# Attention, layer norm and a routed feed-forward on one core: three loads moved, a gate's weights packed, a layer norm's statistics and scaling moved

## The reference, cut to what matters

```python
def _L0_attn_ref(x, Wq, bq, Bq, Aq, ...):          # x is (2, 1024, 512), 16 heads of 32
    q, k, v = lora_linear(x, ...) for each          # x @ W + b + 0.5 * (x @ B) @ A
    attn = softmax(q @ k / sqrt(32), axis=-1)
    return lora_linear(attn @ v, Wo, bo, Bo, Ao)

def _moe(x, Wg, W1, W3, W2, sw1, sw3, sw2):        # 2048 tokens, 8 experts, 256 slots each
    probs = softmax(xt @ Wg); eidx = argmax(probs); gate = probs[eidx]
    pos = place of the token among those of its expert; keep = pos < 256
    h = silu(xd @ W1) * (xd @ W3); oe = h @ W2      # per expert, on the tokens it holds
    out = oe of the token's slot * gate * keep
    return out + silu(xt @ sw1) * (xt @ sw3) @ sw2  # the shared expert, on all tokens

x = layernorm(x + attn(x))
x = layernorm(x + moe(x))
```

## Time and profile before

| | |
|---|---|
| time, median of three runs | 1094.25 us (1091.41 to 1097.25) |
| the profiled execution | 1093.02 us, its span 1091.4 us |
| busy | PE 1041.3 us (95%), DVE 724.1 (66%), ACT 557.3 (51%), POOL 540.3 (50%) |
| granted TensorE clock, mean | 0.989 of full speed |
| chain that ended last | PE 78%, DVE 7%, DMA 4%, issue 4%, ACT 4%, SP's queue 2% |

### The profile page before, as it was taken

One profiled execution on the slowest core, in us unless ns is written; L12 is line 12 of the kernel. 1 busy time (PEld: TensorE's weight loads), 2 busy tenths in 40 slices (PEclk: granted clock), 3 DMA queues, 4 the chain that ended last, 5 costly groups with the idle time before them and its releaser, 6 DMA issues.

```text
span 1091.4 us, 16143 instructions
## 1 busy us (share of the span) xinstructions
PE 1041.3 (95%) x5586; PEld 726.8 (67%) x5586; DVE 724.1 (66%) x1194; ACT 557.3 (51%) x978; POOL 540.3 (50%) x294
## 2 busy tenths in 40 slices
PE   6999999999999999999999988968999999999996
PEld 5777555455555545556445567756899999998884
DVE  5549878878687787888887576512476666664154
ACT  4311556656466565666665654411355656664116
POOL 2100788889878898788889830370000000003600
PEclk9999999999999999999999999989999999999998
DMA  7964342724337142332641492350277777765704
GB/s 265 306 180 136 83 112 56 174 65 95 78 78 175 49 111 55 78 97 51 169 154 63 124 287 72 117 139 18 70 211 214 215 239 229 222 201 125 112 1 154
DMA packets 163765, 146.79 MB, mean 134 GB/s; under 512 B 42529, under 2 KB 126753, under 8 KB 163440
## 3 DMA queue, kind: packets, MB, share of 16 engines
q1 hardware_dynamic: 157040, 129.97, 42.8%
q0 software_dynamic: 6656, 15.93, 5.3%
HBM read 85.75 MB, written 35.67 MB: 111 GB/s over the span
## 4 chain that ended last, share of the span: by engine, by line
PE 78%; DVE 7%; DMA 4%; issue 4%; ACT 4%; SPq 2%; ACTq 0%; DVEq 0%
PE bank L812 16%; PE bank L964 13%; PE bank L977 11%; PE bank L912 11%; PE bank L900 8%; PE bank L1109 8%; PE bank L1022 4%; PE bank L872 3%; PE bank L989 3%; DMA raw<-in_L_ffn_W_dram 2%; DVE w2lo L1735 1%; DVE mx L1606 1%; DMA bcol<-in_L_attn_bk_dram 1%; PE bank L819 1%; DVE sa L1742 1%
## 5 line engine op out<-in xcount | busy, mean ns | idle before, releaser
L1336 ACT ACTIVATE prob<-bank 128x512 f32<-128x512 f32 x512 | 289.9, 597 | 194.3 <-PE bank L964 186.3
L1606 DVE TENSOR_REDUCE mx<-bank 128x1 f32<-128x512 f32 x512 | 324.9, 680 | 81.5 <-PE bank L912 78.6
L740 POOL TENSOR_TENSOR psum<-psum,prob 128x1024 f32<-128x1024 f32 x156 | 366.8, 2388 | 1.0 <-ACT prob L1336 1.0
L964 PE MATMUL bank<-Qs,Ks 97*128 97x512 f32 x512 | 209.0, 424 | 0.9 <-DMA Qs<-mrow 0.9
L912 PE MATMUL bank<-Ks,Qs 96*128 96x512 f32 x512 | 184.6, 405 | 3.8 <-DVE mx L1606 1.3
L964 PEld LDWEIGHTS bank<-Qs,Ks 97*128 97x128 f32 x512 | 94.3, 188 | 106.3 <-ACT prob L1336 74.3
L791 POOL DMA_DIRECT2D oe_d<-oe_sb x16 | 8.8, 548 | 248.8 <-ACT oe_sb L1474 247.8
L977 PE MATMUL bank<-prob,V 128*32 128x512 f32 x1024 | 131.4, 602 | 0.0
L912 PEld LDWEIGHTS bank<-Ks,Qs 96*128 96x128 f32 x512 | 97.2, 190 | 50.2 <-DVE mx L1606 21.8
L740 POOL TENSOR_TENSOR psum<-prob,prob 128x1024 f32<-128x1024 f32 x32 | 76.0, 2394 | 67.8 <-ACT prob L1336 37.8
L900 PE MATMUL bank<-xThi,Wsl 128*128 128x512 f32 x256 | 99.6, 400 | 3.8 <-DMA bcol<-in_L_attn_bk_dram 3.1
(11 more groups left out here) (251 smaller groups left out, 2067.9 us busy)
## 6 DMA issues: line engine op xcount, KB each, us to landing
raw<-in_L_ffn_W_dram SPq DMA_DIRECT2D x120, 256.0 KB
Ks<-plane_khi SPq DMA_DIRECT2D x64, 128.0 KB, 2.7
Qs<-plane_qhi SPq DMA_DIRECT2D x64, 128.0 KB, 2.3
raw<-in_L_ffn_sw_dram SPq DMA_DIRECT2D x30, 256.0 KB
xin<-in_L_attn_x_dram SPq DMA_DIRECT2D x16, 256.0 KB, 5.0
v_d<-v_sb POOLq DMA_DIRECT2D x16, 256.0 KB, 3.9
Wsl<-wt_d SPq DMA_DIRECT2D x16, 256.0 KB, 4.7
Ks<-plane_klo SPq DMA_DIRECT2D x32, 128.0 KB, 2.5
```

Of the source, the lines that this page charges most:

```text
L740: po.tensor_tensor(psum[:, pr], (prob[0] if kc == 1 else psum)[:, pr], prob[kc % RING][:, pr], ALU.add).then_inc(sem("sum_done"), 1)
L964: nc.tensor.matmul(score_at(v, i), Ks[v.b][0:97, hh, kc * P:(kc + 1) * P], Qs[v.b][0:97, hh, v.hf * HALF:(v.hf + 1) * HALF], start=True, s ...
L1336: ACTV(prob[kc % RING][:, hh, :], score_at(v, i), ACT.Exp, scale=SCALE).then_inc(sem("exp_done"), 1)
L1606: ins = RED(mx[(hf + ahead) % 2][:, 4 * hh + qt, part:part + 1], src, AX.X, ALU.max)
```

## The change

There are three edits.

1. `load_slot` for the next group is no longer issued by SP in slot 1, behind pair 1, the load of V and the store of the attention output, but in slot 0, between pair 0 and the row of maxima.
2. The gate's weights are one tile `wgp` of 128 columns: the high part in columns 0 to 7, the low part in columns 8 to 15. `logits` is two matmuls for each of four blocks (turned tile high, turned tile low), 8 in place of 12, into 16 rows; the logits are transposed with 16 columns per tile, and VectorE adds the two parts (one operation more).
3. Statistics of tiles 8 to 11 are taken by VectorE behind the remainders of the turned tiles 0 to 7 and no longer between the residual adds; `x1` of tiles 8 to 15 is done by VectorE and no longer by ScalarE; and the turned tiles 0 to 7 go through five banks and no longer three.

```diff
@@ wgp
-    wgp = [gate(f"wgp{s}", [P, DC, P], FR) for s in ("hi", "lo")]
-    lgT = gate("lgT", [E, T], F32)
+    wgp = gate("wgp", [P, DC, P], FR)
+    lgT = gate("lgT", [2 * E, T], F32)
@@ x1_bank
-        return bank[(2, 3, 5)[t % 3]]
+        return bank[(2, 3, 5, 6, 7)[t % 5] if t < NT // 2 else (2, 3, 5)[t % 3]]
@@ SP: stack_unit, half
             stack(b, 0, 0)
             if v is not None:
+                group = v.g + v.h // 4
+                if v.slot == 0 and group < NG - 1:
+                    load_slot(value((group + 1) * P))
                 next_mrow(v)
...
-            elif v.proj and v.slot == 1:
-
-                c, need = value((v.g + 1) * P), value(v.projected())
-                sp.wait_ge(sem("pj_done"), need)
-                load_slot(c)
@@ GpSimd
-        for s in range(2):
-            po.memset(f32(wgp[s][:]), 0.0).then_inc(sem("wgp_zero"), 1)
+        po.memset(f32(wgp[:]), 0.0).then_inc(sem("wgp_zero"), 1)
@@ TensorE: turn_x1, logits
                 pe.wait_ge(sem("x1_rdy"), t + 1)
-                if t >= 3:
-                    pe.wait_ge(sem("x1_lo"), t - 2)
+                if t == 4:
+                    pe.wait_ge(sem("at_done"), 4 * NG + 1)
+                if t >= 5:
+                    pe.wait_ge(sem("x1_lo"), t - (4 if t < NT // 2 else 2))
                 turn(x1_bank(t), rows(t)).then_inc(sem("x1_t"), 1)
...
-            pe.wait_ge(sem("x1_lo"), 4 * i + 4)
+            pe.wait_ge(sem("x1_lo"), max(4 * i + 4, 5))
             if i >= 2:
                 pe.wait_ge(sem("lg_ev"), i - 1)
-            elif i == 0:
-                pe.wait_ge(sem("at_done"), 4 * NG + 1)
-            split3(bank[6 + i % 2], lambda a, dc: wgp[a][:, dc, :],
-                   lambda p, dc: xT[p][:, dc, i * 512:(i + 1) * 512]).then_inc(sem("lg_full"), 1)
+            for dc in range(DC):
+                for p in range(2):
+                    mm = nc.tensor.matmul(bank[6 + i % 2], wgp[:, dc, :], xT[p][:, dc, i * 512:(i + 1) * 512],
+                                          start=dc == 0 and p == 0, stop=dc == DC - 1 and p == 1)
+            mm.then_inc(sem("lg_full"), 1)
...
-            mm = nc.tensor.transpose(bank[6][:, t * E:(t + 1) * E], lgT[:, t * P:(t + 1) * P], ident[0:E, 0:E])
+            mm = nc.tensor.transpose(bank[6][:, 2 * t * E:2 * (t + 1) * E], lgT[:, t * P:(t + 1) * P], ident[0:2 * E, 0:2 * E])
@@ ScalarE
-        x1_hi(3, 4)
+        x1_hi(3, 8)
         root(2, 8, 12)
-        x1_hi(4, 8)
-        x1(2, 8, 12)
         take_logits(0)
         conv(13, 0, 0, None)
         x1_hi(8, 11)
         root(3, 12, NT)
         x1_hi(11, 12)
-        x1(3, 12, NT)
         take_logits(1)
@@ VectorE
+        def x1(k, start, stop):
+
+            ve.wait_ge(sem("ln_shift"), k)
+            for t in range(start, stop):
+                TS(rows(t), rows(t), ln_scale[:, t:t + 1], ln_shift[:, t:t + 1], ALU.mult,
+                   ALU.add).then_inc(sem("x1_rdy"), 1)
...
-        nc.vector.tensor_copy(r3["lg"][:], by_t(bank[6])).then_inc(sem("lg_read"), 1)
+        parts = bank[6][:, 0:2 * NT * E].rearrange("p (t s e) -> p t s e", s=2, e=E)
+        nc.vector.tensor_copy(r3["lg"][:], parts[:, :, 1]).then_inc(sem("lg_read"), 1)
         ve.wait_ge(sem("lg_read"), 1)
+        TT(r3["lg"][:], parts[:, :, 0], r3["lg"][:], ALU.add).then_inc(sem("lg_read"), 1)
+        ve.wait_ge(sem("lg_read"), 2)
```

More of the change, by code:

```diff
@@ L1382, in wgp_split @@
         def wgp_split():
-            ac.wait_ge(sem("wgp_zero"), 2)
+            ac.wait_ge(sem("wgp_zero"), 1)
             ac.wait_ge(sem("wg_ld"), 16)
-            ACTV(wgp[0][:, :, 0:E], wg_raw[:], ACT.Identity).then_inc(sem("wgp_hi"), 1)
+            ACTV(wgp[:, :, 0:E], wg_raw[:], ACT.Identity).then_inc(sem("wgp_hi"), 1)
         def x1_hi(start, stop):
@@ L1392, in take_logits @@
             ac.wait_ge(sem("lg_full"), i + 1)
-            ACTV(lgT[:, i * 512:(i + 1) * 512], bank[6 + i % 2][0:E, :], ACT.Copy).then_inc(sem("lg_ev"), 1)
+            ACTV(lgT[:, i * 512:(i + 1) * 512], bank[6 + i % 2][0:2 * E, :], ACT.Copy).then_inc(sem("lg_ev"), 1)
         def conv(kind, c, sets, need):
@@ L1690, in tile, with statistics @@
             TT(rows(t), o_bank(t), xr[t % 4][:], ALU.add).then_inc(sem("y_done"), 1)
+            if t // 4 != 2:
+                statistics(t)
+        def statistics(t):
             ve.wait_ge(sem("y_done"), t + 1)
@@ L1750, in _ @@
             tile(t)
-        variances(8, 12)
         x1_rest(0, 3)
         ve.wait_ge(sem("wgp_hi"), 1)
-        TT(wgp[1][:, :, 0:E], wg_raw[:], f32(wgp[0][:, :, 0:E]), ALU.subtract).then_inc(sem("wgp_lo"), 1)
-        x1_rest(3, 4)
+        TT(wgp[:, :, E:2 * E], wg_raw[:], f32(wgp[:, :, 0:E]), ALU.subtract).then_inc(sem("wgp_lo"), 1)
+        x1_rest(3, 8)
+        for t in range(8, 12):
+            statistics(t)
+        variances(8, 12)
         scales(2, 8, 12)
-        x1_rest(4, 8)
+        x1(2, 8, 12)
         for t in (12, 13):
@@ L1766, in _ @@
         scales(3, 12, NT)
+        x1(3, 12, NT)
         x1_rest(11, NT)
```

## The result

| | before | after |
|---|---|---|
| time, median of six runs | 1094.9 us (1091.41 to 1097.25) | 1086.47 us (1082.96 to 1087.57) |
| ratio | | 0.991 [0.9887, 0.9933] |
| the profiled execution, its span | 1093.02, 1091.4 us | 1086.6, 1085.0 us |
| TensorE busy | 1041.3 us (95%) | 1038.3 us (96%) |
| at tile 11's residual add | 641.84 | 637.70 |

8.4 us less between the medians; the forecast was 1084, its range 1078.5 to 1090.5. The last three lines read as a ledger of the two profiled executions: the lead is 4.14 us at the end of attention, 6.88 at the shared expert's first chunk, 8.76 at the transposition of the logits, and 6.4 at the end. The profiled execution of the kernel before was 1.9 us quicker than its median and that of the change was at its median, so the 8.4 of the medians and the 6.4 of the spans do not contradict each other.

A forecast was written before the change was run, and what follows sets the result against it. TensorE, busy 95% of the span, was taken as the bound. 4.8 + 1.8 + 3.0 = 9.6 us off 1093.02 (profiled) or 1094.25 (median) gave 1083.4 or 1084.7, forecast 1084; 8-in-10 range 1078.5 to 1090.5.

The forecast's parts named there:

- rival (a): VectorE/GpSimd port collisions cost full price (0.7) and TensorE's clock falls ahead of `up(0, ...)` (about 1.3): 1086; chance 0.14.
- Edit 1, 4.8: Attention, slot 1: moving the slices removes TensorE's bias waits, 4.0 us in group 1 and 0.8 in group 2.
- SP's delay of 0.1: SP's queue, slot 0: six moved issues against 3.9 us of slack delay what follows by 0.1 us, hidden.
- Rival (b): SP is held up in the new place: 3 x 2.9 = 8.7 us lost, 1093, no change; chance 0.06.
- Edit 2, 1.8: Gate logits: fewer matmuls save 1.9 us in TensorE's lone stretch, less 0.1 for transpositions; VectorE's extra operation hidden.
- Edit 3 with logits 0 and 1, 3.0: Between attention and routing: VectorE's new order starts the shared expert's first chunk 3.0 us earlier.
- the dear one: Behind attention: scales and scalings on VectorE both wait for GpSimd's adds, leaving 2.3 us won at the first chunk.
- a sign of being wrong: VectorE behind attention: scalings or scales of over 1 us each beside GpSimd's adds would show the forecast wrong.
- between the last two: First chunk's gain: 3.0 us, chosen between 3.4 (only small scale operations wait) and 2.3 (scalings wait too).
- The port: VectorE and GpSimd block each other at a shared port pair; by it scalings collide and the sum uses 2.3.
- What follows moves as a whole: Shared expert and experts, behind routing: they start earlier by the whole gain; the 28.5 us of ScalarE waits taken unchanged.
- Rival (c): Gain of the gate and VectorE-order edits is hidden by VectorE's delay or ScalarE's waits: 1089; chance 0.09.

The follow-up runs named there:

- gate_only: Kernel before with only the gate's low-part weights made eight more columns of one tile (fewer logits matmuls): 1093.15 us, 0.9982.
- add15_behind: Changed kernel with GpSimd's residual add for tile 15 waiting until VectorE has scaled tiles 8 to 11: one run, 1089.96 us.
- slices_only: Kernel before with only the next group's weight slices issued in slot 0 instead of slot 1: 1092.4 us, 0.9982.
- order_only: Kernel before with only the late statistics, scalings of tiles 8 to 15 on VectorE and five banks: 1091.2 us, 0.9968.
- scale8_act_conv_late: Changed kernel with scaling of tiles 8 to 11 back on ScalarE and a VectorE conversion moved behind tile 14: 1082.25 us, 0.9887.
- no_gate_scatter: Changed kernel without the 16 indirect DMAs that write the gates, so the gates are zero: 1068.86 us, 0.9757.
- before_gates_in_norm: Kernel before without the gates' scatter, full result through row scaling by 1/gate and the layer norm: 1077.72 us, 0.9994 on the third chip.

## Why the prediction was right

The time was 1086.5 where 1084 was forecast, 8.4 us won where 9.6 were summed. The ledger of the two traces has 8.76 for the same sum. The time is nearest to rival (a), 1086, and half of that rival came: the port collisions took their full price. Its other half, a further fall of the clock that would make `up(0, ...)` slower, didn't (its first 24 matmuls take 5.59 us, 0.233 each), so that the time agrees with (a) is in part luck. By the steps:

- **Edit 1, 4.8.** The first wait and the slow clock behind it gave 4.0 us (15.33 against 19.35), and the second 1.0, the predicted 4.0 and 0.8. At the end of attention only 4.14 stand. In between, TensorE's timeline shows two short idle times for which no releaser is seen: 1.27 us ahead of 324.82, where it was 0.81 before, and 0.89 ahead of 519.13, where nothing was. They were not foreseen, and the edit alone isn't their cause: gate_only, which doesn't have it, shows both, and longer. With them the term is 0.7 short in the two traces, the largest miss of the sum. In the medians it may be more: the prediction took the wait's price from one execution in which the clock fell behind it, and in two of the four traced kernels without the edit it doesn't, where the term is 3.0 to 3.4 and not 4.8. The 2.3 measured for the edit alone, up to 3.8 by its interval, fits that; how often the clock falls there isn't known from four traces. SP's delay of 0.1 was 0.16, hidden as said; six issues cost 4.1 us (3.95 in group 0), and the row of maxima had that much slack and no more, as the doubled load shows. Rival (b) was not far away.
- **Edit 2, 1.8.** 14.00 - 12.12 = 1.88, the transpositions cost the same 1.10, VectorE's further operation is hidden. Right to a tenth.
- **Edit 3 with logits 0 and 1, 3.0.** 6.88 - 4.14 = 2.74. The pieces are right one by one: the low part of the gate's weights at 0.18 (0.2 taken), `logits(0)` 4.3 us behind the end of projection 11 (642.00 - 637.66; 4.6 said), a wait of 2.68 ahead of turning tile 11 (2.5), and the clock's fall behind it, hidden since the next turning waits for VectorE all the same. The case that came is the dear one, the scales and the scalings both held up by GpSimd: 1.14 for 0.16, and 3.19 for 1.91, 2.3 us in all; single operations of 1.14 and 1.80 us are also what the prediction had named as a sign of being wrong. My price for that case, 2.3 us won, was lower than the 2.74 that came, so 0.4 of the delay found slack that I hadn't counted; where isn't traced. The chosen 3.0, "between the last two", was on the optimistic side of the two collisions.
- **The port.** The Trainium skill (SBUF — State Buffer, "SBUF: two separate sides") has VectorE and GpSimd exclude each other; by the prediction's reading of it the scalings count. The rows agree, 3.19 against 1.91 us with nothing changed but GpSimd's add (add15_behind). Moving them to ScalarE won 1.4 us up to the first chunk in the trace. The medians, 1086.47 and 1084.08, are 2.4 us apart, but their intervals against the kernel before, [0.9887, 0.9933] and [0.9883, 0.9915], overlap.
- **What follows moves as a whole.** Nearly so in the medians (8.4 of 8.76), and less in the two profiled executions, where 8.76 became 6.46. Half of that loss lies in the stretch of the earlier trace rows, where the lead goes from 8.8 to 7.5 us: ScalarE's waits are 28.4 for 28.5 in all and TensorE's idle time is 13.3 for 13.1, but its clock is 0.81 for 0.86. The other half, 1.0, lies between 865 and 975 us, among the experts, where the chain goes through the weight loads. Neither is a loss that every gain meets: against the kernel before, slices_only loses 0.1 us across the stretch and order_only nothing, and among the experts slices_only gains 0.7 and scale8_act_conv_late 0.9. So the term of 0 for what follows holds to about 1 us at each of the two places, and what differs there isn't traced further. Rival (c) has no support in these rows. What the prediction couldn't say of the waits is why they are there; on the chip of no_gate_scatter, 17.6 us hang on the gates' scatter.

## What to carry to other kernels

A load may be moved ahead in a DMA queue as far as the queue's slack before the next urgent copy covers its issues; work it out in issue times (0.6 to 0.7 us each here), since one set of six more cost 16.6 us in three groups. When work goes to VectorE, look at what GpSimd does in the same microseconds: two adds there cost 2.3 us, and the freed ScalarE was idle. And when a term is a wait and the lower clock behind it, price it with and without the fall: of four executions with nearly the same wait two had it. Compare two traces from a place up to which the kernels are the same, or the accidents of one execution are read as a cause.

## What the runs showed that was not expected

- The same kernel takes 1095 us on two chips and 1077 on a third. Taking 16 small indirect writes away is worth 17.6 us on one of the former; taking them away and scaling rows instead is worth nothing on the latter.
- An operation of VectorE on 4 columns takes 1.14 us and not 0.16 beside one add of GpSimd, and one scaling 1.80 and not 0.55: in proportion the smallest instructions lose the most.
- The length of TensorE's idle time alone doesn't say whether the granted clock falls. Behind 2.30 us it was 0.55 for 3.6 us (the kernel before, 282.4) and behind 2.68 it was 0.51 (661.1); behind 2.52 at the same wait it stayed at 1.00 (before_gates_in_norm, 280 to 290). Behind 1.60 us ahead of 330.74 in gate_only it fell all the same, to 0.50 from 332.2 to 335.6; behind 1.09 in scale8_act_conv_late it did not.
